# Expert tiles' rows turned by transfers, three rotating diagonals and a new written order in a fused attention and expert kernel

## What is computed

```
x = x + xattn(_layernorm(x), ctx, ctx)      # per token: scores 16 x 16, mask tril, softmax, out 16 x 16
h = _layernorm(x);  top1 = argmax(h @ gate_w.T + gate_b)
y_e = relu(h @ w1[e].T + b1[e]) @ w2[e].T + b2[e]
x = x + y_[top1]
```

## Time and profile before

| what | us |
|---|---|
| median of 3 runs | 477.7 (477.31 to 478.84) |
| span of the profiled execution, first to last instruction | 492.6 |
| PE busy in it | 402.1 (82%) |
| DVE / POOL / ACT busy | 346.3 / 208.7 / 177.5 |
| first `ups` matmul | 241.1 |
| last store issued | 485.5 |

### The profile page before, as it was taken

How to read it: one execution, slowest core, us unless ns; L and a number is a source line. 1 busy time by engine, 2 the same in 40 slices (tenths; PEclk the granted TensorE clock), 3 DMA queues, 4 the chain that set the end, 5 groups by cost and what they waited for, 6 DMA issues and landing times.

```text
span 492.6 us, 16316 instructions
## 1 busy us (share of the span) xinstructions
PE 402.1 (82%) x5967; PEld 338.3 (69%) x5967; DVE 346.3 (70%) x777; ACT 177.5 (36%) x317; POOL 208.7 (42%) x213
## 2 busy tenths in 40 slices
PE   0135868888888866897999999779999999999992
PEld 0025757887787765896887877557778877877871
DVE  7978969789945863477757877457666666766662
ACT  3343255542624221342434433224333333433420
POOL 8345374334673467523723242642333323233221
PEclk9999999999999999975699999889999999999998
DMA  8999578899685664377612232544333322222210
GB/s 282 414 305 218 135 170 241 212 259 260 160 220 119 152 167 107 106 173 181 207 45 67 68 76 81 185 131 155 90 68 77 77 62 62 69 60 61 84 31 0
DMA packets 105162, 69.39 MB, mean 141 GB/s; under 512 B 78077, under 2 KB 88190, under 8 KB 104576
## 3 DMA queue, kind: packets, MB, share of 16 engines
q1 hardware_dynamic: 75696, 56.67, 41.9%
q10 hardware_dynamic: 25984, 3.21, 4.6%
q0 software_dynamic: 3408, 8.46, 4.6%
HBM read 48.28 MB, written 12.57 MB: 124 GB/s over the span
## 4 chain that ended last, share of the span: by engine, by line
PE 55%; DMA 11%; SPq 9%; DVE 9%; issue 6%; POOL 5%; ACT 2%; ACTq 1%; another core or an unknown queue 1%; POOLq 0%; DVEq 0%
PE s_ps L1229 20%; SPq L305 8%; PE at_ps L1245 6%; DMA arena<-qv_hl 6%; PE pv_ps L1245 6%; PE pv_ps L1143 6%; PE s_ps L1111 3%; PE lg_ps L1171 3%; PE pv_ps L1246 3%; PE at_ps L1246 3%; POOL qv_hl L987 2%; PE tr_ps L1156 2%; DMA arena<-x 2%; PE st_ps L1196 2%; POOL k_hl L995 1%
## 5 line engine op out<-in xcount | busy, mean ns | idle before, releaser
L1229 PEld LDWEIGHTS s_ps<-arena 128*128 x1872 | 132.7, 99 | 52.2 <-issue 14.6
L1229 PE MATMUL s_ps<-arena 128*128 128x128 f16 x1872 | 158.6, 222 | 8.4 <-DVE arena L906 5.1
L915 DVE SCALAR_TENSOR_TENSOR arena<-arena,s_ps 128x512 f32<-128x512 f32 x78 | 53.6, 687 | 48.6 <-PE s_ps L1229 35.9
L1076 POOL DMA_INDIRECT result<-arena x39 | 38.8, 995 | 95.5 <-DVE arena L940 91.6
L1111 PEld LDWEIGHTS s_ps<-k_hl,arena 128*128 128x128 f16 x1536 | 54.3, 118 | 29.9 <-DMA arena<-qv_hl 22.1
L1111 PE MATMUL s_ps<-k_hl,arena 128*128 128x16 f16 x1536 | 54.7, 179 | 23.3 <-DMA arena<-qv_hl 19.3
L1143 PE MATMUL pv_ps<-a_hl,arena 128*128 128x16 f16 x1536 | 54.7, 179 | 19.7 <-DMA arena<-qv_hl 15.9
L1143 PEld LDWEIGHTS pv_ps<-a_hl,arena 128*128 128x128 f16 x1536 | 53.5, 118 | 22.8 <-DMA arena<-qv_hl 18.3
L1245 PE MATMUL at_ps<-arena,k_in 128*128 x160 | 60.9, 383 | 0.8 <-DVE k_hl L926 0.6
L1245 PE MATMUL pv_ps<-arena,x_in 128*128 x152 | 58.1, 383 | 0.1
L1069 POOL TENSOR_TENSOR arena<-arena 128x256 f32<-128x256 f32 x39 | 30.7, 786 | 60.7 <-DMA arena<-b 60.6
(11 more groups left out here) (143 smaller groups left out, 614.2 us busy)
## 6 DMA issues: line engine op xcount, KB each, us to landing
arena<-w SPq DMA_DIRECT2D x28, 512.0 KB, 6.1
arena<-sorted_rows SPq DMA_DIRECT2D x39, 130.0 KB, 2.4
arena<-b SPq DMA_DIRECT2D x39, 128.0 KB
arena<-qv_hl SPq DMA_DIRECT2D x70, 64.0 KB, 3.5
k_in<-k_t SPq DMA_DIRECT2D x16, 256.0 KB, 3.9
v_in<-v_t SPq DMA_DIRECT2D x16, 256.0 KB
arena<-x SPq DMA_DIRECT2D x4, 1024.0 KB, 12.1
o_sb<-x_r SPq DMA_DIRECT2D x16, 256.0 KB, 3.8
```

Of the source, the lines that this page charges most:

```text
L915: eng.scalar_tensor_tensor(out=h_in[:, c].rearrange("p (k t) -> p k t", t=P), in0=bias, scalar=W_SCALE, in1=h_ps[c][:].rearrange("p (k t) ...
L1076: eng.indirect_dma_start(out=out, out_offset=bass.IndirectOffsetOnAxis(ap=rows[:, r, :].bitcast(I32)[:, D + 2:D + 3], axis=0), in_=rows[:, ...
L1229: k = eng.matmul(o, weights_of(j, w + k_ * H + n * P, P), xt[:, j % 2, k_ * P:(k_ + 1) * P], start=k_ == 0 and w is HI_1 and xt is xt_hi, ...
```

## The change

1. **Tile inputs.** The two float32 transposes of each tile on PE go. ACT normalises as before to `xn2`, then copies it, still row by row, to the high half in `x2_hl`; DVE subtracts for the low half beside it; one DMA transpose of 128 x 512 float16 (128 KB) on SP's queue turns both halves from `x2_hl` into `xt`, which has 4 buffers (`XB`). `x2_hl` lies where `a_hl` was, so tile 0 now waits for the last outputs of the attention. `rows` gets 8 buffers. `h_in` moves to the slot of `v_flat`, and the new value of a half waits for that half of tile j-1 to have been taken by `rests`.
2. **Diagonals.** Three diagonals rotate: chunk i uses diagonal i mod 3 first for its queries and, when its scores are made, for its values. Queries and values go in transfers of their own, all of 32 KB, 16 per chunk in place of 8: values of chunk i wait for the scores of chunk i, queries of chunk i+3 for the outputs of chunk i.
3. **Order.** `weave` takes its times from a table `TIMES`, one list per engine and generator, the formula of the tiles included. Two memsets of diagonals are exchanged between DVE and POOL; the last expert's w1 is loaded after the outputs of chunk 14, not after the last scores; tile 0's fetch waits for one chunk's outputs less.

```
+TIMES = {
+    "SP": {
+        "load_x": (80, 118, 2562, 3151, 4287, 4640, 7466, 7819, 8525, 9245, 12320, 12711, 13417, 13665, 16787, 17140,),
...
-def weave(*lanes):
+def weave(times, **lanes):
+    turns = sorted((t, n, k) for n, name in enumerate(lanes) for k, t in enumerate(times[name]))
...
-        q_bd = diagonals[:, 2 * SLOT_BLOCKS:], diagonals[:, 0:SLOT_BLOCKS]
-        v_bd = [q_bd[0] if i == NC - 2 else diagonals[:, SLOT_BLOCKS:2 * SLOT_BLOCKS] for i in range(NC)]
+        SIDES = 3
+        diagonal = [diagonals[:, n * SLOT_BLOCKS:(n + 1) * SLOT_BLOCKS] for n in (1, 2, 0)]
...
-        FR = 6
+        FR, XB = 8, 4
...
-        xt_hi = carve(q_flat, 2 * D).rearrange("p (n c) -> p n c", n=2)
-        xt_lo = carve(q_flat, 2 * D).rearrange("p (n c) -> p n c", n=2)
-        h_in = carve(q_flat, 4 * HALF).bitcast(F32).rearrange("p (n c) -> p n c", n=2)
+        xt = carve(q_flat, XB * 2 * D).rearrange("p (n c t) -> p n c t", n=XB, t=P)
+        x2_hl = a_hl[:].rearrange("p n a q -> p (n a q)").rearrange("p (r c) -> p r c", r=2)
+        h_in = v_flat[:, 0:4 * HALF].bitcast(F32).rearrange("p (n c) -> p n c", n=2)
...
-        def spread_part(eng, i, n):
+        def spread_part(eng, i, n, halves_of):
             part, cols = slice(HD * n, HD * (n + 1)), slice(HEADS * n, HEADS * (n + 1))
-            at = slice(1 - i % 2, 3 - i % 2)
-            if i + 2 < NC:
-                to = diagonals[part, at.start * SLOT_BLOCKS:at.stop * SLOT_BLOCKS, cols]
-                eng.dma_start(to, qv_hl[part, at].rearrange("p s b c u a -> p (s b) c u a")).then_inc(s_bd[i % 2], 16)
-            else:
-                eng.dma_start(v_bd[i][part, :, cols], v_hl[part]).then_inc(s_bd[i % 2], 16)
+            eng.dma_start(diagonal[i % SIDES][part, :, cols], halves_of[part]).then_inc(s_bd[i % SIDES], 16)
...
+            def spread_queries():
+                for i in range(NC):
+                    yield
+                    if i < SIDES:
+                        sp.wait_ge(*((s_zero_0, 1), (s_zero, 1), (s_zero, 2))[i])
+                    else:
+                        sp.wait_ge(s_pv, i - SIDES + 1)
                     sp.wait_ge(s_q_hi, i + 1)
                     sp.wait_ge(s_q_lo, i + 1)
+                    for n in range(8 - LATER):
+                        spread_part(eng, i, n, q_hl[i % 2])
+            def spread_values():
+                for i in range(NC):
+                    yield
                     sp.wait_ge(s_v_hi, i + 1)
                     sp.wait_ge(s_v_lo, i + 1)
+                    sp.wait_ge(s_qk, i + 1)
                     for n in range(8 - LATER):
+                        spread_part(eng, i, n, v_hl)
...
+            def turn_rows():
+                for j in range(NTILES):
+                    yield
+                    sp.wait_ge(s_x2_hi, j + 1)
+                    sp.wait_ge(s_x2_lo, j + 1)
+                    sp.wait_ge(s_up, 2 * (j - XB + 1))
+                    eng.dma_start_transpose(xt[:, j % XB], x2_hl[:, j % 2]).then_inc(s_xt[j % XB], 16)
...
-                    act.wait_ge(s_xt2, j + 1)
-                    act.wait_ge(s_up, 2 * (j - 1))
-                    eng.copy(xt_hi[:, j % 2], xt2_ps).then_inc(s_xt_hi, 1)
+                    act.wait_ge(s_pv, NC)
+                    act.wait_ge(s_xn2, j + 1)
+                    if j >= 2:
+                        act.wait_ge(s_xt[(j - 2) % XB], 16 * ((j - 2) // XB + 1))
+                    eng.copy(x2_hl[:, j % 2, 0:D], xn2).then_inc(s_x2_hi, 1)
...
-                    dve.wait_ge(s_xt_hi, j + 1)
-                    dve.wait_ge(s_up, 2 * (j - 1))
-                    eng.tensor_tensor(xt_lo[:, j % 2], xt2_ps, xt_hi[:, j % 2], ALU.subtract).then_inc(s_xt_lo, 1)
+                    dve.wait_ge(s_x2_hi, j + 1)
+                    eng.tensor_tensor(x2_hl[:, j % 2, D:2 * D], xn2, x2_hl[:, j % 2, 0:D], ALU.subtract).then_inc(s_x2_lo, 1)
...
-            def expert_inputs():
-                for j in range(NTILES):
-                    yield tile_at(j) + 0.6
-                    pe.wait_ge(s_q, NC)
-                    pe.wait_ge(s_xn2, j + 1)
-                    pe.wait_ge(s_xt_lo, j)
-                    for k_ in range(KD):
-                        k = eng.transpose(xt2_ps[:, k_ * P:(k_ + 1) * P], xn2[:, k_ * P:(k_ + 1) * P], ident[:])
-                    k.then_inc(s_xt2, 1)
...
-                            pe.wait_ge(s_xt_lo, j + 1)
-                            pe.wait_ge(s_xt_hi, j + 1)
+                            pe.wait_ge(s_xt[j % XB], 16 * (j // XB + 1))
```

More of the change, by code:

```diff
@@ L1248, in downs @@
                     k.then_inc(s_down, 1)
[L1250 removed]
+            weave(TIMES["PE"], statistics=statistics(), gate_columns=gate_columns(), scores=scores(),
+                  turned=turned(), outputs=outputs(), turned_outputs=turned_outputs(), gates=gates(),
+                   ups=ups(), downs=downs())
 def kernel(x, ctx_1024, L0_ffn_gate_w, L0_ffn_gate_b, L0_ffn_w1, L0_ffn_b1, L0_ffn_w2, L0_ffn_b2):
```

505 lines of the change are left out of this document (281 added, 224 removed), and 105 rows, old and new, of tables (TIMES, act, op1).

## The result

| | us, median | lowest to highest | span of the profiled execution |
|---|---|---|---|
| before | 478.27 (4 runs) | 477.31 to 481.20 | 492.6 |
| changed | 511.13 (4 runs) | 509.67 to 514.56 | 508.3 |

The changed kernel takes 1.067 times as long, 95% interval 1.062 to 1.073. I had forecast 472, faster; it is slower by 33 us, outside the range.

The account below looks back on a forecast made before the run. PE waits about a fifth of the attention and bounds the steady tiles. Changes of -5.4 and -0.6 at the end made -6.0: span 486.6, times 0.970, 472 us; own range 466 to 476, 8 in 10 from 457 to 488.

Parts of the forecast that it names:

- Part 1, "I take -4": Attention: values no longer waiting for earlier outputs save 4 us, a quarter of the visible waits of 15.9.
- the queue has room: Attention: SP's queue, 110 us of block transfers plus about 50 of loads, fits in 208 us.
- PE waits for the diagonals above 42: Attention: sign that small issues in SP's queue bind it, together with SP running without gaps.
- Part 2, the gates: Before tile 0: gate blocks add 5.5 us and cover a 5.4 us input wait; first `ups` at 242.6.
- Part 2, the loop, "17.3 / 3 = 5.77 a tile": Steady tiles: the input loop over three tiles, with 3.8 us transpose landing, sets 5.77 us a tile, against 5.53 before.
- Part 2, the stalls: Expert tiles: of some 16 us of stalls and turned outputs, 6 remain, giving 225.3 us for the tiles.
- These 4.2 go: Tile 17: its fetch no longer stands right behind the last fill, so a 4.2 us stall disappears.
- The sum: Whole kernel: -5.4 and -0.6 at the end give -6.0, span 486.6, time 472 us.
- The factor of 0.970: Whole kernel: profiled span times 0.970 (477.7 / 492.6) gives the timed median.
- queue rival: Attention: the queue of small issues binds it, +12 in place of -4, span 502.6, time 487; chance 0.09.
- quick rival: Tiles: transposes land in 2.4 us, PE sets the pace at 5.3 us a tile, time 457.5; chance 0.26.

Follow-up runs that it names:

- before_again: The kernel before, profiled anew with nothing changed, on chip 7: 503.3 us in a single run.
- after_again: The changed kernel with nothing altered, run again on chip 1: 529.8 us, 1.064 times the kernel before.
- pe_turns: The changed kernel with tile inputs turned on PE in float32 as before, its new order otherwise kept: 526.9 us, 1.061 times the kernel before.
- graft2: The kernel before with DMA-transposed tile inputs, eight row buffers, fetches 17.2 us ahead, inputs 5.3 ahead, last gate blocks before tile 0: 481.1 us, 0.958 times before.
- graft: The kernel before with DMA-transposed tile inputs placed earlier, eight row buffers, fetches 11.5 us ahead, fills 2.0 us apart: 518.3 us, 1.036 times before.
- inputs_ahead: The changed kernel with tile input steps 4.5 us earlier and fetches 9 us earlier, from tile 2 on: 518.8 us, 1.037 times the kernel before.

## Why the prediction was wrong

**What bounds the kernel.** Right: an attention in which PE waits, tiles in which PE is the bound.

**Part 1, "I take -4".** This step failed by most. The attention got 11 us longer in the two first profiles, 13.8 from before_again to after_again, and 14.5 on chip 7 by pe_turns, whose attention is the changed one (252.0 for 237.5). I had a mechanism (45 us more issuing in SP's queue) and its price (+12), and put it at 0.09 because "the queue has room". In the old order the number of transfers is shown as the cause (12.4 of 13.4 come back with 64 fewer); in the changed kernel's own order fewer transfers give back 5.4, and the other 8 stay open. The room was a mean again: SP's waits from 36 to 236 are 81.7 us in before_again and still 43.8 in after_again, but the issues come in groups of five to ten at the moments when a load or the next group is wanted. The gain I set against it was real as a wait (24.0 to 8.6) and worth nothing as time, since the softmax took its place. My sign for this rival ("PE waits for the diagonals above 42") was wrong too: the loss appears under POOL's and DVE's names.

**Part 2, the gates.** "First `ups` at 242.6", with 5.5 for the gates and the transfer covered by them: the gates cost 4.9 of shift (15.9 less 11.0) and covered the transfer. Right.

**Part 2, the loop, "17.3 / 3 = 5.77 a tile".** Measured 5.97 over the last 16 tiles of the first profile. The loss per tile came out, 0.25 for the forecast 0.24, because before takes 5.72 over the same tiles and not 5.53 (three of its steps there take 6.4 to 6.5, which my 5.53 left out); that is luck, as the terms of my loop were wrong. The landing was no worse than I took (3.2 for 3.8), the issue was 1.24 for 0.7. What was missing was SP's queue: I let the transpose's issue hold what stands behind it and did not ask what stands ahead of it. With the 7.0 of the chain above in place of 3.9 the same loop would give (13.4 + 7.0) / 3 = 6.8 for a tile so placed; only some are (PE waits for seven transposes, 9.7 us), and 5.97 is the mean. The Trainium skill ("Advanced Engine Details and Errata", X-Bar Transpose (TRN2)) calls these transfers as fast as regular ones. For the landing the trace agrees roughly (3.2, and 2.8 in graft2, against 2.5 for the fetch and 3.1 for the biases of 128 KB); for the issue it does not, 1.24 against 0.33 for the fetch, and the measurement decides.

**Part 2, the stalls.** This is the step that failed in the tiles: I let about 16 us of stalls shrink to 6, and they did not. "These 4.2 go": at tile 17 they do, but the fills moved to tiles 12 to 14, whose steps are 8.1, 8.9 and 10.4 us in the first profile: fills between 320.83 and 345 stand ahead of transposes and fetches in SP's queue. From tile 8 to tile 17 both kernels take the same, 63.1 and 62.5.

**The sum.** Forecast -6.0 in the span; measured +15.7: the attention +11 for -4 is 15 of the difference, the tiles 233.6 for 225.3 are 8.3, and some 1.6 go the other way in the gates and at the end. The factor of 0.970 from span to time was wrong as well: it held for the one profile of before, and the changed kernel's profiled execution has a time of 510.04 for a span of 508.3. That is the rest of the 33 us between the times; where it lies in the stages the first two profiles cannot tell.

**The rivals.** No rival stood alone: the queue rival came true in the attention by its size, +11 for +12, and the tiles lost too, by the queue and the stalls and not by a slow landing. I treated the rivals as exclusive, though both can come from more issues in SP's queue. The queue rival's 16 above the forecast and the 8 measured in the tiles give 486.6 + 16 + 8 = 511 on the profile, near 508.3; the 8 is no forecast of mine. The quick rival's gain was real, and came only with another order: graft2.

## What to carry to other kernels

Count a queue's issues by the moment, not by the mean: in a queue that takes its work in order, 0.6 us each delays everything behind it; in the old order here a quarter fewer transfers gave back far more than half the bytes. When a step becomes a transfer, write down the whole loop through the issuing queue, with what stands ahead of it, and place loads far enough ahead that no load waits behind a transfer which itself waits for a load. A wait removed is worth time only if nothing else is due at that moment; ask which engine's name the time will take.

## What the runs showed of the hardware

A DMA transpose of 128 KB from buffer to buffer takes 1.24 us of SP's queue, twice the 0.61 of a 32 KB copy in the same kernel and nearly four times the 0.33 of a fetch of 130 KB from HBM; its landing (2.8 to 3.2 us) is ordinary. I expected the reverse, a cheap issue and a slow landing.

The same kernel takes 478 to 487 us on one chip and 494 to 511 on four others, a larger step than most edits here; the ratio of the changed kernel, each time taken on one chip, held (1.067 and 1.064).

PE can stand for no reason that the profile names: in graft the last outputs come in pieces of four matmuls with about 0.5 us between, two rows of PE's timeline:

```profile
237.17 0.29 PE L1168 MATMUL pv_ps<-a_hl,arena 128*128 128x16 f16 x4 [0.48 <-issue]
237.90 0.29 PE L1168 MATMUL pv_ps<-a_hl,arena 128*128 128x16 f16 x4 [0.43 <-issue]
```

What causes it was not tried. Open as well: the 8 us that the new order keeps in the attention when issues or bytes are taken away, PE's 11.8 us of waits for DVE's rests in inputs_ahead, and whether the split transfers would cost less on another queue than SP's.
